# Second attention of a fused decoder kernel: probabilities as the stationary operand, row sums as matmul columns, outputs transposed by DMA, keys paired on VectorE

## The reference

```python
def _L1_xattn_ref(query, key, value, Wq, Wk, Wv, Wo):
    # 32 query heads, 8 key/value heads (each repeated 4 times), head size 16
    scores = jnp.einsum('bqhd,bkhd->bhqk', q, k) * scale
    probs = jax.nn.softmax(scores, axis=-1)
    out = jnp.einsum('bhqk,bkhd->bqhd', probs, v)
    out = out.transpose(0, 2, 1, 3).reshape(b, sq, DIM)
    return out @ Wo
...
x = x + _L1_xattn_ref(_layernorm(x, axis=-1), ctx_4096, ctx_4096, L1_xattn_Wq, L1_xattn_Wk, L1_xattn_Wv, L1_xattn_Wo)
```

## Time and profile before

| what | value |
|---|---|
| median of 3 runs | 1663.84 us (1663.59 to 1664.19) |
| span of the profiled execution | 1663.4 us |
| TensorE, VectorE, ScalarE, GpSimd busy | 1510.4, 1273.3, 789.3, 289.0 us |
| second attention's loop over tiles | from 1410.09 us to about 1580 us |
| transposes issued in it | 64 of 128 x 1024 elements |

### The profile page before, as it was taken

How to read it: one execution, slowest core, us unless ns; L and a number is a source line. 1 busy time by engine, 2 the same in 40 slices (tenths; PEclk the granted TensorE clock), 3 DMA queues, 4 the chain that set the end, 5 groups by cost and what they waited for, 6 DMA issues and landing times. The chain is left out here.

```text
span 1663.4 us, 29998 instructions
## 1 busy us (share of the span) xinstructions
PE 1510.4 (91%) x11382; PEld 803.7 (48%) x11398; DVE 1273.3 (77%) x2386; ACT 789.3 (47%) x1677; POOL 289.0 (17%) x249
## 2 busy tenths in 40 slices
PE   5799999999999999999999987799999998787695
PEld 4455455555555555555555543344444544344353
DVE  6577667667677667767776786899999986999777
ACT  3343433424334243342333332566777763888652
POOL 2001002001011011011011001111211103789620
PEclk7799999999999999999999998899999999899898
DMA  7031231321312212221312112122222350767402
GB/s 265 1 78 51 68 85 26 79 75 43 98 39 66 76 52 64 68 61 52 77 51 62 48 70 102 23 45 45 45 44 44 58 117 1 140 107 123 79 1 101
DMA packets 273838, 113.48 MB, mean 68 GB/s; under 512 B 239154, under 2 KB 255539, under 8 KB 273460
## 3 DMA queue, kind: packets, MB, share of 16 engines
q1 hardware_dynamic: 234820, 78.67, 21.6%
q10 hardware_dynamic: 38896, 33.03, 6.3%
HBM read 44.57 MB, written 11.53 MB: 34 GB/s over the span
## 5 line engine op out<-in xcount | busy, mean ns | idle before, releaser
L627 PE MATMUL xp<-WO,OT 128*128 128x512 f16 x1536 | 341.1, 382 | 5.6 <-DVE X L824 5.6
L585 PE MATMUL pj<-XT,WQ 128*128 128x512 f16 x1536 | 339.0, 381 | 6.4 <-PEq L379 6.4
L627 PEld LDWEIGHTS xp<-WO,OT 128*128 128x128 f16 x1536 | 148.2, 98 | 189.3 <-issue 18.4
L585 PEld LDWEIGHTS pj<-XT,WQ 128*128 128x128 f16 x1536 | 148.4, 98 | 182.3 <-DVE WKV L294 6.7
L705 ACT ACTIVATE E<-E 128x512 f32<-128x512 f32 x64 | 40.1, 627 | 329.0 <-DVE E L801 329.0
L824 DVE SCALAR_TENSOR_TENSOR X<-xp,X 128x512 f32<-128x512 f32 x128 | 88.2, 690 | 113.0 <-PE xp L627 112.0
L565 POOL TENSOR_TENSOR VW<-VW,XB 128x1024 f32<-128x1024 f32 x14 | 32.9, 2351 | 769.8 <-DVE VW L107 769.8
L1028 PE MATMUL db<-W0T,XD 128*128 128x448 f16 x768 | 162.2, 363 | 0.0
L1045 PE MATMUL eb<-W1T,DT 128*128 128x512 f16 x672 | 147.7, 380 | 4.2 <-ACT EB L1120 2.5
L766 DVE SCALAR_TENSOR_TENSOR QT<-pj,QT 128x512 f16<-128x512 f32 x128 | 88.0, 687 | 67.9 <-ACT QT L688 67.6
L1028 PEld LDWEIGHTS db<-W0T,XD 128*128 128x128 f16 x768 | 76.9, 100 | 74.7 <-issue 8.0
(11 more groups left out here) (236 smaller groups left out, 2427.0 us busy)
## 6 DMA issues: line engine op xcount, KB each, us to landing
W0T<-in_L_xattn_wq ACTq DMA_DIRECT2D x7, 1024.0 KB, 5.3
W0T<-in_L_xattn_wo ACTq DMA_DIRECT2D x7, 1024.0 KB, 5.0
CS<-in_ctx SPq DMA_DIRECT2D x4, 1024.0 KB, 10.1
X<-in_x SPq DMA_DIRECT2D x4, 1024.0 KB, 11.2
out<-X SPq DMA_DIRECT2D x8, 512.0 KB, 3.6
XB<-in_L_ffn_W ACTq DMA_DIRECT2D x28, 128.0 KB, 2.8
w0t<-XB ACTq DMA_DIRECT2D x7, 512.0 KB, 3.3
w1t<-W0T ACTq DMA_DIRECT2D x7, 512.0 KB, 3.8
```

Source lines behind the costliest of these rows:

```text
L585: last = pe.matmul(bank[:, :], w, src[:, b, k, tokens], start=n == 0, stop=n == 3 * KC - 1)
L627: last = pe.matmul(xp[i % 2][:, :], OT[:, a, j, i * P:(i + 1) * P], WO[:, b, j, :], start=n == 0, stop=n == 3 * REP - 1)
```

## The change

- **Weighing turned round.** In `weigh_values` the transposed probabilities (128 x 128) are now stationary and the values move, 34 columns: 2 heads x 16 and two columns that sum the probabilities of the two key groups. Tokens now lie on partitions of the output, in two banks (ob, rt). `sums`, `reciprocals` of the sums, `widen`, `spread` and `spread_out` go; `normalise` takes two reciprocals of 16 elements and two products of 256 from PSUM. VM has 34 columns, its two sum columns are set to 1 once by GpSimd, and it has four buffers in place of two.
- **Outputs transposed by DMA.** `high_out` and `low_out` write OS (tokens on partitions), and SP issues four DMA transposes a tile, 128 x 256 each, into OT (`turn_out`), behind the probabilities' transposes of the next tile. `project_out` waits for them.
- **Keys paired on VectorE.** `pair_keys` moves from GpSimd (one TENSOR_TENSOR) to VectorE (two TENSOR_SCALARs), the mask `odd` is now F32.
- **Order.** QT and OT are interleaved by pairs of heads. TensorE: scores, transposes, project, turn_weights, weigh_values(t-1), project_out(t-2). `weigh_values(t-1)` waits for `low_x(t+8)`, whose bank it takes; `low_x` moves in between the maxima; `transposes(t+8)` waits for `normalise(t-2)`. ScalarE places values two tiles ahead and does `high_out(t-1)` last; GpSimd normalises one tile further ahead and does `low_out(t-1)` last.

```diff
         @block.sync
         def _(sp):
+            def turn_out(t):
+                if t >= 2:
+                    sp.wait_ge(S["xp_done"], t - 1)
+                for part, split in enumerate(("ot_hi", "ot_lo")):
+                    sp.wait_ge(S[split], t + 1)
+                    to = OT[:, t % 2, part, :, :, :].rearrange("p u (b t) j -> p b u (t j)", b=2)
+                    for b in range(2):
+                        sp.dma_start_transpose(to[:, b, :, :], OS[:, part, b * 2 * P:(b + 1) * 2 * P]).then_inc(S["od_done"], 16)
+
...
+                if t >= 1:
+                    turn_out(t - 1)
                 if t == 1:
                     sp.wait_ge(S["o_lo"], 1)
                     load_weights2(sp)
+            turn_out(TILES - 1)
...
             def low_out(t):
                 pool.wait_ge(S["ot_hi"], t + 1)
...
+                if t >= 1:
+                    pool.wait_ge(S["od_done"], 64 * t)
+                pool.tensor_tensor(OS[:, 1, :], ON[:, :], OS[:, 0, :], ALU.subtract).then_inc(S["ot_lo"], 1)
...
             def weigh_values(t):
+
                 pe.wait_ge(S["vm_done"], t + 1)
-                pe.wait_ge(S["on_done"], t)
-                if t == 0:
-                    pe.wait_ge(S["tp_lo"], AHEAD)
+                pe.wait_ge(S["on_done"], 2 * t)
+                pe.wait_ge(S["tp_lo"], min(t + 1 + AHEAD + 1, TILES))
                 for h in range(2):
                     pe.wait_ge(S[f"pt{h}_done"], 32 * t + 32)
                 for b in range(2):
-                    for n, (va, pa) in enumerate(PASSES):
+                    for i in range(2):
                         for q in range(4):
-                            last = pe.matmul(ob[q * 32:(q + 1) * 32, b * 256:(b + 1) * 256], VM[:, t % 2, va, b, q, :],
-                                             PT[t % 2][:, pa, q, 2 * b:2 * b + 2, :], start=n == 0, stop=n == 2)
-                last.then_inc(S["ot_done"], 1)
+                            for n, (pa, va) in enumerate(PASSES):
+                                last = pe.matmul(weighed(b)[:, i * 4 + q, :], PT[t % 2][:, pa, q, 2 * b + i, :],
+                                                 VM[:, t % 4, va, b, q, :], start=n == 0, stop=n == 2)
+                    last.then_inc(S["ot_done"], 1)

             def project_out(t):
-                pe.wait_ge(S["ot_lo"], t + 1)
+                pe.wait_ge(S["od_done"], 64 * t + 64)
...
-                    last = pe.matmul(xp[:, :], OT[:, t % 2, a, j, :], WO[:, b, j, :], start=n == 0, stop=n == 3 * REP - 1)
+                    last = pe.matmul(xp[:, :], OT[:, t % 2, a, j // 2, :, j % 2], WO[:, b, j, :], start=n == 0, stop=n == 3 * REP - 1)
...
             for t in range(TILES + 2):
                 if t < TILES:
                     scores(t)
-                if 1 <= t <= TILES:
-                    spread(t - 1)
+                if t + AHEAD < TILES:
+                    transposes(t + AHEAD)
                 if t + REP < UNITS:
                     project(t + REP)
-                if t + AHEAD < TILES:
-                    transposes(t + AHEAD)
                 if t in W_SLOT:
                     turn_weights(W_SLOT[t])
+                if 1 <= t <= TILES:
+                    weigh_values(t - 1)
                 if t >= 2:
                     project_out(t - 2)
-                if 1 <= t <= TILES:
-                    weigh_values(t - 1)
...
             for t in range(TILES + 3):
-                if 1 <= t <= TILES:
-                    widen(t - 1)
-                if 2 <= t < TILES + 2:
-                    high_out(t - 2)
+                if t + AHEAD < TILES:
+                    high_x(t + AHEAD)
                 if t >= 3:
                     out_x(t - 3)
+                if t + 2 < TILES:
+                    place_values(t + 2)
...
+                for h in range(2):
+                    dve.tensor_scalar(KM[:, t % 2, :, h, :], KT[:, :, t * P:(t + 1) * P], odd[:, h:h + 1], None,
+                                      ALU.mult).then_inc(S["km_done"], 1)
...
                     if q:
                         less_max(t, q - 1, s3[q - 1])
+                    if q == 2 and t + AHEAD < TILES:
+                        low_x(t + AHEAD)
                 less_max(t, 3, s3[3])
...
             def normalise(t):
-                dve.wait_ge(S["ot_done"], t + 1)
-                dve.wait_ge(S["r_out"], t + 1)
+                for b in range(2):
+                    dve.wait_ge(S["ot_done"], 2 * t + b + 1)
+                    dve.reciprocal(RC[:, 2 * b:2 * b + 2, :].rearrange("p u (q g) -> p (u q) g", g=2),
+                                   weighed(b)[:, :, 2 * HEAD1:VCOLS]).then_inc(S["rcp_done"], 1)
                 if t >= 1:
                     dve.wait_ge(S["ot_lo"], t)
-                dve.tensor_tensor(ON[:, :], ob[:, :], RS[:, :], ALU.mult).then_inc(S["on_done"], 1)
+                for b in range(2):
...
```

More of the change, by code:

```diff
@@ L1306, in attention1 @@
         _, _, KT, V, project_kv1, high_kv1, low_kv1 = kv1
-        QT = [sb(ph, f"QT1_{i}", [P, 2, BB, REP, SEQ], F16) for i in range(2)]
+        QT = [sb(ph, f"QT1_{i}", [P, 2, BB, 2, SEQ, 2], F16) for i in range(2)]
         XT = [sb(ph, f"XT1_{i}", [P, 2, KC, BLOCK], F16) for i in range(2)]
@@ L1428, in _ @@
             pool.memset(VM[:, :, :, :, :, :], 0.0).then_inc(S["mask_done"], 1)
-            pool.wait_ge(S["mask_done"], 5)
-            pair_keys(0)
-            for n in range(6, AHEAD):
+            pool.wait_ge(S["mask_done"], 6)
+            for h in range(2):
+                pool.memset(VM[h * SEQ:(h + 1) * SEQ, :, 0, :, :, 2 * HEAD1 + h:2 * HEAD1 + h + 1], 1.0).then_inc(S["mask_done"], 1)
+            pool.wait_ge(S["mask_done"], 8)
+            for n in range(6, AHEAD + 1):
                 normal(n)
-            pair_keys(1)
             def split_bias(n):
@@ L1459, in _ @@
                     zero_last()
[L1460 to L1461 removed]
                 if t >= 3:
                     add_x(t - 3)
[L1464 to L1465 removed]
+                if t + AHEAD + 1 < TILES:
+                    normal(t + AHEAD + 1)
                 if t < TILES:
@@ L1468, in _ @@
                         low_probs(t, q)
-                if t + 2 < TILES:
-                    pair_keys(t + 2)
+                if 1 <= t <= TILES:
+                    low_out(t - 1)
         @block.tensor
@@ L1689, in _ @@
                     high_probs(t, 1)
-                if 1 <= t <= TILES:
-                    spread_out(t - 1)
+                if t + REP < UNITS:
+                    high(t + REP)
                 if t < TILES:
@@ L1696, in _ @@
                     high_probs(t, 3)
-                if t + REP < UNITS:
-                    high(t + REP)
-                if t + AHEAD < TILES:
-                    high_x(t + AHEAD)
                 if t in W_SLOT:
@@ L1704, in _ @@
                     stats_scalar(act, 3, (0,))
-                if t + 1 < TILES:
-                    place_values(t + 1)
+                if 1 <= t <= TILES:
+                    high_out(t - 1)
             stats_scalar(act, 3, (1,))
@@ L1748, in bias_rows, with pair_keys @@
                     dve.tensor_copy(BS[row, :], BH[row, n, :]).then_inc(S["oh_done"], 1)
+            def pair_keys(t):
+                if t == 0:
+                    dve.wait_ge(S["mask_done"], 5)
+                if t >= 2:
+                    dve.wait_ge(S["sc_done"], t - 1)
+                if t == AHEAD:
+                    dve.wait_ge(S["kv_lo"], 4)
+                for h in range(2):
+                    dve.tensor_scalar(KM[:, t % 2, :, h, :], KT[:, :, t * P:(t + 1) * P], odd[:, h:h + 1], None,
+                                      ALU.mult).then_inc(S["km_done"], 1)
             def scores_less_max(t):
@@ L1806, in _ @@
                     scores_less_max(t)
-                    sums(t, 0)
-                    sums(t, 1)
-                    reciprocals(t)
                 if t + REP < UNITS:
                     low(t + REP)
-                if t + AHEAD < TILES:
-                    low_x(t + AHEAD)
+                if t + 2 < TILES:
+                    pair_keys(t + 2)
                 if t in W_SLOT:
```

104 lines of the change are left out of this document (38 added, 66 removed).

## The result

The changed kernel takes 1705.93 us (median of 4 executions, 1704.49 to 1709.64); the kernel before, on the same chip, 1664.01 (1663.59 to 1665.26). The ratio is 1.0248, 95% interval 1.0233 to 1.0263: 42 us slower, outside the range of 1652 to 1684. The profiled execution spans 1703.8 us against 1663.4, so 40.4 us have to be found.

What follows compares the result with a forecast made beforehand. It took a ring over ScalarE, GpSimd, TensorE and VectorE to bound the second attention. Start -1.0, tiles -1.9, +2.1 and +2.8, clock +1 and tail +2 gave +5.0: 1668.8 us, eight in ten within 1652 to 1684.

Steps and rivals of the forecast that it cites:

- What leaves; VectorE's sum: Second attention: VectorE loses two row sums and a reciprocal, and with the additions needs 7.7 us a tile, from 9.6.
- Key pairing, 0.2 each: On VectorE: each of the two new TENSOR_SCALARs of 256 f16 elements takes 0.2 us, bounds 0.1 and 0.42.
- Weighing 1.55: On TensorE: weighing as 48 matmuls with own loads takes 1.55 us a tile, +0.8; upper bound 2.9.
- rival 3: TensorE: light weighing matmuls leave the clock at half in steady tiles, about +2.5 us a tile, 1698 us; chance 0.05.
- Issue of a small transpose, 0.95: On SP: issuing one 128x256 output transpose takes 0.95 us, read off a line through two larger sizes; bounds 0.6 and 1.28.
- 0.15 late, which GpSimd's part hides: SP queue: the next tile's probabilities transpose waits only 0.15 us behind the last output's issue, hidden by GpSimd's part.
- The DMA path, 6.6 from the low parts' end: SP and DMA: probabilities' issue 1.75, three outputs at 0.95, landing 2.0: 6.6 us, giving 9.8 us a tile.
- Rival 2: Output transposes: the DMA path is long, 9.4 us, so 11.2 us a tile and 1688 us in all; chance 0.15.
- Clock, +1 (0 to +4): TensorE, tiles 12 to 17: idling brings two more projections at half clock, counted half, +1 us.
- The sum by stretch: Whole kernel: start -1.0, tiles 3 to 8 -1.9, 8 to 12 +2.1, 12 to 15 +2.8, clock +1, tail +2 us.
- The second ring: Scores, VectorE's operations, weighing, projection: 8.8 us a tile, deciding only if the DMA path is over 2 us shorter.
- rival 1: Output transfers are short, 4.5 us in place of 6.6: about -11 us, 1653 us; chance 0.30.

Runs made afterwards that it cites:

- Experiment 7: The changed kernel without output transposes (projecting from zeros), with the output projection ahead of the weighing on TensorE: 1652.93 us, 0.9923 of the kernel before.
- experiment 12: The changed kernel, its four small output transposes kept, with the output projection one tile later and ahead of the weighing: 1698.91 us, 1.0203 of the kernel before.
- experiment 3: The kernel before with four idle 128x256 DMA transposes a tile added on SP, their result never read: 1691.63 us, ratio 1.0157.
- experiment 8: The changed kernel with six useless matmuls a tile while TensorE waits for the outputs, to hold the clock up: 1699.66 us, 1.0202 of the kernel before.
- experiment 4: The changed kernel without its output transposes, outputs projected from zeros (that part of the computation left out): 1663.24 us, 0.9987 of the kernel before.
- experiment 10: The changed kernel with one 128x1024 output transpose a tile, projection one tile later and ahead of the weighing: 1657.91 us, 0.9957 of the kernel before.

## Why the prediction was wrong

The direction was the likelier of the two as forecast (slower, 0.48). The size was not: +5 against +42. That the sign came out is partly luck: the +5 was the outputs' path at 9.8 us a tile with the queue's own period at nothing, and what the runs show is that period. By its own steps:

- **What leaves; VectorE's sum.** Right. VectorE has 48.56/6 = 8.1 us a tile with holes (forecast 7.7), of the difference 0.4 for the pairing.
- **Key pairing, 0.2 each.** Right alone (four in 0.86 us), but 0.82 for the two beside GpSimd in most tiles and 1.90 in the last: at 1512.53 the first takes 0.625, to 0.07 behind the end of GpSimd's instruction, and the second adds 0.2. I had bounds for the instruction, not for its neighbour. In the changed kernel this is not on the path.
- **Reciprocals 0.25, half normalisations 0.42.** Measured 0.22 (mean of 0.24 and 0.19) and 0.42.
- **Weighing 1.55.** Measured 1.35 (1508.94 to 1510.29). The light matmuls did not cost more than their row said (28 ns a pair). The sign that the prediction set for rival 3, a projection of over 4 us before tile 8, did come (4.6 to 5.3 us), but behind waits and not by these matmuls: in experiments 7 and 12 they are the same, and the first nine projections last 2.75 to 2.77 us.
- **Writes with a step of two, 0.** The projections' copies rose from 0.58 to 0.72 us on ScalarE and from 0.69 to 0.74 on VectorE; they are off the path here.
- **Issue of a small transpose, 0.95: the step that failed first.** I drew a line through 1.23 at 1024 columns and 1.52 at 1792 and read it at 256. Measured 1.24 (1.23 at 128, 1.26 at 512): flat up to 1024, so that the 0.85 read off for zero columns has no row behind it. The bound of 1.28 was in the text; the value taken was the line's.
- **"0.15 late, which GpSimd's part hides": the step that failed worst.** I followed the outputs' path to its end and never summed SP's own period. The rows were there: the probabilities' four issues, one of them pushed back, 3 x 1.23 + 2.41 = 6.1, and four outputs at 1.28 with the same push, 6.2, make 12.3 us, and with one push in the eight 11.2. Even at 0.95 each the sum is 9.9, above the 9.8 us that I gave the tile. A queue that is only 0.15 late is a queue without room; it should have been the bound, and the 11.5 measured are its sum. Experiments 3 and 12 show it full whatever waits for what: SP waits 0.6 and 2.7 us for other engines in 161.
- **The DMA path, 6.6 from the low parts' end.** From the start of the last probabilities' issue (1499.61 + 5.38 - 1.28 = 1503.7) to the projection at 1512.37 it is 8.7. Rival 2 had 9.4, and 11.2 us a tile, 1688 in all, 18 short: its price per tile was near, its mechanism (a long path, with a landing of 3.2) was not. The landing measured 2.4, and experiment 12 gives it a tile of room for 7 us. It also lacked the clock.
- **Clock, +1 (0 to +4).** The projection waits in every tile and not only from 12 on, 0.3 to 4.5 us, in 13 of 16 tiles 2 us or more, and 12 projections ran at 4.2 to 5.3 us. Experiment 8 puts this at 6 us net, most of it ahead of tile 3.
- **The sum by stretch.** Scores of tile 3 at 1443.00 in place of 1437.5; tiles 3 to 8 62.56 us (forecast 49.0); 8 to 12 44.22 (38.8); 12 to 15 38.02 (28.7); tail 30.2 (28). The misses are 5.5, 13.6, 5.4, 9.3 and 2.2 us.
- **The second ring, 8.8 us a tile, if the transfers were short (rival 1, 1653).** Experiment 4 is that case at its best and took 1663.2. In tiles 4 to 8 it ran at 8.9, as worked out; in tiles 12 to 15 it lost the gain again. I had the weighing wait for the probabilities of tile t-1 and found them landed at 5.05, well ahead; that holds at 9.8 us a tile and no longer at 8.8 or below, where every us the tile gets shorter brings the weighing nearer to them. Experiment 7 gives that back: 10.3 us.
- **Readings.** The landing of 4.6 behind the 5.05 isn't in the earlier trace rows, whose nearest is 4.9; that makes 5.35 and decides nothing. By the text's own sum the second ring (8.8) decides below a DMA path of 4.6, not of 5.4 as rival 1 has it; the measured path was far from both.

So the account: the output transposes are all of the 42 us (experiment 4). By place, in the profiled execution, 4.5 us lie before the scores of tile 3, 31.2 between tiles 3 and 15 (144.8 against 113.6) and 4.2 in the tail. Twelve tiles at the 11.4 us of a full queue (experiment 3) would be 137, so an estimate from these numbers gives the queue 23 of the 31. The other 8, and the tail, are waits in the path through the queue and half clock, not told apart further; experiment 8 puts the clock at 2.5 there and 4.2 ahead of tile 3. The 26.6 of experiment 3 and the 6 of experiment 8 can't be added, since experiment 3 has half clock of its own. Beneath, without the transposes, the change's own order of weighing and projection hid 10.3 of 12 us (experiments 4 and 7). The best complete kernel, experiment 10, is 7.5 us below the kernel before.

## What to carry to other kernels

Sum each issuing queue over one period, as one does for each engine, and count DMA transposes by number before bytes: here eight a tile filled the queue at 11.4 us, while with five it waited 34 us of 133 for the probabilities. A queue that comes out "just late" is the bound. When a step gets a slower input, ask both how many tiles of room its consumer has and what is queued behind that consumer: the later projection gained 13 us, the swapped order alone lost 13, both together gained 21.

## What was not expected of the hardware

- The issue of a DMA transpose between 128 and 1024 columns costs SP the same: 1.23, 1.24, 1.26, 1.28 us; at 1792 it is 1.54. Landing is 2.4 us at 128 and 256 columns, 2.5 at 512, 3.1 to 3.3 at 1024 (medians in the stream).
- One of four transposes in quick succession takes 2.2 to 2.4 us to issue. From 1500 to 1546 of experiment 8 SP pauses for up to 1.2 us, no output's issue takes over 1.25, and the period stays at 11.4.
- With five issues a tile the DMA engines' share is 0.99 to 1.02, at 157 to 169 GB/s.
- An f16 tensor_scalar of 256 elements on VectorE takes 0.28 us beside an idle GpSimd and up to 2.03 beside a busy one, and ended 0.07 to 0.08 behind GpSimd's instruction where it was looked at.
